# Who starts the first loads: weights on SP, biases and first rotary tables on ACT, two groups of dummy matmuls fewer

## The reference, cut to what matters

```
q = rope(x @ Wq + bq); k = rope(x @ Wk + bk); v = x @ Wv + bv      # 16 heads of 16
ctx = softmax(q k^T / 4) v
x = layernorm(x + ctx)
r = sigmoid(xr @ W_r^T); k = relu(xk @ W_k^T)^2; x = layernorm(x + r * (k @ W_v^T))
```

## Time and profile before

| | before |
|---|---|
| median of 3 runs | 1515.15 us (1514.39 to 1572.35) |
| profiled execution, its time | 1515.05 us |
| its span, first to last instruction | 1513.0 us |
| mean granted TensorE clock | 0.999 |
| PE busy | 1501.9 us, 99% |
| DVE, ACT, POOL busy | 1348.6, 1190.2, 347.0 us |

### The profile page before, as it was taken

How to read it: one execution, slowest core, us unless ns; L and a number is a source line. 1 busy time by engine, 2 the same in 40 slices (tenths; PEclk the granted TensorE clock), 3 DMA queues, 4 the chain that set the end, 5 groups by cost and what they waited for, 6 DMA issues and landing times.

```text
span 1513.0 us, 49359 instructions
## 1 busy us (share of the span) xinstructions
PE 1501.9 (99%) x21956; PEld 679.9 (45%) x21956; DVE 1348.6 (89%) x1453; ACT 1190.2 (79%) x2179; POOL 347.0 (23%) x348
## 2 busy tenths in 40 slices
PE   9999999999999999999999999999999999999998
PEld 3344444444444444444444444444444444443476
DVE  5669999999999999999999999999999999998597
ACT  3338888888888888888888888888888888888845
POOL 3510322132212212132213221042212000000175
PEclk9999999999999999999999999999999999999999
DMA  7825111121112100121112111101111212000133
GB/s 220 256 75 173 22 23 24 24 79 24 24 24 79 24 11 15 24 79 24 24 24 79 24 24 24 67 15 24 23 24 24 38 24 35 5 3 3 30 75 120
DMA packets 71957, 73.14 MB, mean 48 GB/s; under 512 B 47745, under 2 KB 57473, under 8 KB 69953
## 3 DMA queue, kind: packets, MB, share of 16 engines
q1 hardware_dynamic: 71200, 69.60, 20.1%
q10 hardware_dynamic: 544, 0.39, 0.1%
HBM read 29.07 MB, written 13.63 MB: 28 GB/s over the span
## 4 chain that ended last, share of the span: by engine, by line
PE 97%; DVE 1%; DMA 1%; ACT 1%; SPq 0%; issue 0%; POOL 0%; POOLq 0%; DVEq 0%; ACTq 0%
PE ring_ps L573 29%; PE score_ps L644 29%; PE pv_ps L592 29%; PE score_ps L547 2%; PE ring_ps L618 2%; PE score_ps L730 2%; PE score_ps L714 1%; PE pv_ps L714 1%; PE pv_ps L547 1%; PE score_ps L558 1%; DMA rope<-tables 0%; ACT probs L819 0%; DVE rope L1084 0%; PE pv_ps L558 0%; PE ring_ps L730 0%; DMA k_stack<-rope 0%
## 5 line engine op out<-in xcount | busy, mean ns | idle before, releaser
L1147 DVE TENSOR_REDUCE tile_max<-ring_ps 128x1 f32<-128x1024 f32 x1024 | 1207.3, 1215 | 116.3 <-PE ring_ps L573 111.2
L819 ACT ACTIVATE probs<-score_ps 128x512 f32<-128x512 f32 x2048 | 1109.9, 598 | 211.6 <-PE score_ps L644 153.5
L644 PE MATMUL score_ps<-q_stack,k_stack 99*32 99x512 bf16 x8192 | 715.5, 379 | 1.8 <-ACTq L807 0.8
L573 PE MATMUL ring_ps<-k_stack,q_stack 96*32 96x512 bf16 x8192 | 625.9, 378 | 0.4 <-DMA k_stack<-rope 0.4
L592 PE MATMUL pv_ps<-probs,v_aug 128*32 128x512 f32 x4096 | 532.0, 591 | 0.0
L573 PEld LDWEIGHTS ring_ps<-k_stack,q_stack 96*32 96x32 bf16 x8192 | 230.9, 96 | 331.1 <-issue 153.1
L644 PEld LDWEIGHTS score_ps<-q_stack,k_stack 99*32 99x32 bf16 x8192 | 227.7, 95 | 326.2 <-issue 150.1
L592 PEld LDWEIGHTS pv_ps<-probs,v_aug 128*32 128x32 f32 x4096 | 129.9, 110 | 98.2 <-ACT probs L819 0.3
L924 POOL TENSOR_TENSOR neg_cuts<-neg_max,zeros 128x16 bf16<-128x16 f32 x31 | 6.8, 219 | 533.8 <-DVE neg_max L1120 533.8
L916 POOL TENSOR_TENSOR v_aug<-v_all,b_v_s 128x256 f32<-128x256 f32 x32 | 23.2, 727 | 298.7 <-PE pv_ps L592 292.8
L937 POOL TENSOR_TENSOR ctx_part<-ctx_turn,recip 128x256 f32<-128x256 f32 x32 | 20.4, 636 | 237.1 <-DVE recip L1179 237.0
(11 more groups left out here) (108 smaller groups left out, 505.7 us busy)
## 6 DMA issues: line engine op xcount, KB each, us to landing
qk_raw<-probs SPq DMA_DIRECT2D x28, 256.0 KB, 3.7
rope<-qk_raw SPq DMA_DIRECT2D x7, 1024.0 KB, 4.8
rope<-qk_raw SPq DMA_DIRECT2D x14, 512.0 KB, 7.3
q_stack<-rope SPq DMA_DIRECT2D x31, 192.0 KB, 3.7
k_stack<-rope SPq DMA_DIRECT2D x31, 192.0 KB, 4.2
xz<-x_tok SPq DMA_DIRECT2D x2, 2048.0 KB, 12.2
q_stack<-rope SPq DMA_DIRECT2D x31, 128.0 KB, 3.7
k_stack<-rope SPq DMA_DIRECT2D x31, 128.0 KB, 3.7
```

Source lines behind the costliest of these rows:

```text
L573: mm = pe.matmul(ring_ps[k % 2][g:g + VCOLS, c * TOK:(c + 1) * TOK], q_stack[0:ROWS, buf, qt * P + g:qt * P + g + VCOLS], k_stack[0:ROWS, ...
L644: mm = pe.matmul(score_ps[n % SCORE_BANKS][g:g + VCOLS, :], k_stack[0:ROWS_M, h % STACKS, kt * P + g:kt * P + g + VCOLS], queries[:, j], s ...
L819: act.activation(probs[:, kt % 2, j, :], score_ps[n % SCORE_BANKS][:, :], ACT.Exp, scale=SCALE).then_inc(exps_done, 1)
L1147: dve.reduce_max(tile_max[:, h % 2, unit // 2, unit % 2:unit % 2 + 1], slot[:, :], AX.X)\
```

## The change

The first weights are no longer issued by ACT but by SP, ahead of everything else. ACT waits until they have landed and then issues the biases and tables 0, which SP issued before. SP's queue has one DMA more at its head and two fewer behind. The dummies go from seven groups of four matmuls to five. Nothing else is touched.

```diff
-WARM_UP = 7
+WARM_UP = 5
...
+            sp.dma_start(w_qk_s[:, :, 0:P], w_first).then_inc(w_first_in, DMA)
             for c, signal in enumerate((x_first_in, x_in[0])):
                 sp.dma_start(x_s[:, 0, c, :], x_blk[0, :, c, :]).then_inc(signal, DMA)
...
             sp.dma_start(w_v_s[:, :, :], w_v).then_inc(w_v_in, DMA)
-            sp.dma_start(b_qk_s[:, :], b_qk).then_inc(b_first_in, DMA)
             load_x(1)
-            load_tables(0)
             load_tables(1)
...
         def _(act):
-            act.dma_start(w_qk_s[:, :, 0:P], w_first).then_inc(w_first_in, DMA)
+            act.wait_ge(w_first_in, DMA)
+            act.dma_start(b_qk_s[:, :], b_qk).then_inc(b_first_in, DMA)
+            act.dma_start(tables_s[:, 0], tables[0]).then_inc(tables_in[0], DMA)
             act.wait_ge(b_first_in, DMA)
```

## The result

The changed kernel took 1517.67 us in the median of 14 runs (1515.73 to 1520.51), the kernel before 1514.95 us in 14 runs beside them. The ratio of the two is 1.0018, with a 95% interval of 1.0011 to 1.0025: slower by 2.7 us. Within the 2% of a "same" this is no change; against my forecast of +0.02 us and a range that ended at 1517.2 it is a miss. The one slow run of before, at 1572.35, is left out of the ratio, and without it the medians differ by 2.9 us.

What follows compares the result with a forecast made beforehand. PE was taken as the bound from the first maximum on, so its start decides: the stacks' wait goes, block 1's grows equally, +0.02 us. With 1515.05 profiled and the median 0.1 higher: 1515.1 us, range 1513.5 to 1517.2.

Steps and rivals of the forecast that it cites:

- What bounds the kernel: Up to the first maximum: PE's own chain and the one through tables 0 meet there, PE's only 0.37 us behind.
- 9.9 for block 1: Token block 1's landing: 9.9 us in place of 9.3, bounds 8.9 to 10.4, as it shares with tables 0.
- I take 9.9: Landing of tables 0 from ACT's queue: 9.9 us in place of 10.55, issued at about 4.5.
- My upper bound of 12.0: Landing of tables 0 on ACT's queue: issue at 4.5 plus the 7.45 us of before.
- Cost: nothing: First weights on SP: block 0 and w_v slide 0.5 to 0.65 us, hidden by the wait for block 1.
- Rival (b): Tables 0 late on ACT's queue, landing near 13.1 behind SP's loads; DVE's chain last, 2.5 us longer: 1517.6 us; chance 0.11.
- The dummies: Start of PE: two groups fewer remove 0.85 us of PE time in front of a wait, worth nothing.
- the sign that I named: PE's item 0 starts near 4.6 at full pace: 16 matmuls in 1.9 us is right, twice that wrong.
- Rival (c): PE's clock rises later; item 0 and first v at 1.2 GHz, first maximum 2.0 us later: 1517.1 us; chance 0.08.
- ACT's waits: Before ACT's first work: biases land at 7.8, 3.8 us after issue; v is ready at 8.5, so nothing is delayed.
- The sum: Whole kernel: 1515.05 profiled plus 0.02, and the median of the runs 0.1 higher: 1515.1 us, 0.0%.
- My last sign of being wrong: Behind 30 us: the prediction is wrong if anything there changes in length.

Runs made afterwards that it cites:

- e5: The kernel before with only the first weights moved, to the head of SP's queue; seven groups of dummies: 1515.54 us, ratio 1.0004.
- e3: The changed kernel with the biases back on SP's queue, behind w_v and ahead of block 1; ACT issues tables 0 alone: 1516.14 us, ratio 1.0008.
- e6: The kernel before with biases and tables 0 issued by ACT once the first weights, still on ACT, have landed; seven groups of dummies: 1518.67 us, ratio 1.0027.
- g2: Second profile of e6, nothing changed against it; a single run: 1518.64 us.
- g3: Second profile of e4, nothing changed against it; a single run: 1517.62 us.
- e4: The changed kernel with the two DMAs on ACT's queue swapped, tables 0 ahead of the biases: 1516.97 us, ratio 1.0012.
- f3: The kernel before, unchanged, run and profiled a second time: 1514.37 us, ratio 0.9995.
- e1: The kernel before with five groups of dummies in place of seven, all loads as before: 1515.76 us, ratio 1.0002.
- f2: The kernel before with two groups of dummies in place of seven, all loads as before: 1514.68 us, ratio 0.9999.
- e8: The changed kernel as it is, profiled a second time: 1517.00 us, ratio 1.0016 to the kernel before.
- g1: The changed kernel as it is, third profile; a single run: 1517.43 us.
- e2: The changed kernel with seven groups of dummies in place of five, its loads kept: 1517.17 us, ratio 1.0011.
- f4: The changed kernel with seven groups of dummies, profiled a second time (first profile: e2): 1517.13 us, ratio 1.0015.
- f1: The kernel before with tables 0 issued by ACT right behind the first weights, with no wait; biases stay on SP: 1514.47 us, ratio 0.9998.
- e7: The kernel before with the biases issued by ACT right behind the first weights, with no wait; tables 0 stay on SP: 1513.99 us, ratio 0.9994.

## Why the prediction was wrong

**What bounds the kernel: right, with some luck in the number.** Two chains meet at the first maximum, and what is late there reaches the end. PE's chain was predicted to 0.1 us (29.27 against 29.36), but its 9.9 for block 1 was reckoned from sharing with tables 0 alone. In e5, where only the first weights had moved, block 1 landed at 9.77 and 9.40, so the move of the weights, which I had put at nothing, was part of the 10.00. In the other two profiles of the changed kernel it was 10.49 and 10.36.

**The step that failed: "I take 9.9" for the landing of tables 0.** It measured 12.00, and 12.22 and 12.58 in the later profiles. Behind it stood an issue at 4.5 and 5.4 us of transfer; the issue came sooner, at 3.73, and the transfer took 8.27 us. I had reckoned that a second queue shares at once and that tables 0 and block 1 would end together, since the bytes ahead are the same. They were not: tables 1, 512 KB, were now issued ahead of tables 0. My upper bound of 12.0 hit the number by two errors that cancel, 4.5 + 7.45 for 3.73 + 8.27. What the runs showed in its place: in the changed kernel tables 0 pair with tables 1 and not with block 1. On one queue the loads of 512 KB land in the order of *issue*, mostly about 1.3 us apart; tables 0 on the other queue land 0.1 to 0.6 us from one that SP issued shortly before or behind them. Issue and landing in four kernels:

| | tables 0 | block 1 | tables 1 | block 2 |
|---|---|---|---|---|
| before | 3.10, 10.55 | 2.62, 9.26 | 3.57, 11.83 | 4.05, 13.11 |
| changed | 3.73, 12.00 | 3.06, 10.00 | 3.53, 11.56 | 4.01, 12.96 |
| e3 | 3.45, 11.29 | 3.52, 11.48 | 3.99, 12.73 | 4.47, 14.01 |
| e6 | 4.34, 14.29 | 2.14, 8.34 | 2.61, 9.60 | 3.08, 11.47 |

The queues do not run to this order by a rule: once the data of tables 0 flow, ACT's queue gets about half (51.6% against 51.3% in e3). And the order across the queues has exceptions: in e6 and g2 tables 0 landed 1.1 us ahead of block 3, and in g3 0.08 us ahead of block 1, though these had been issued 0.2 us before them. The step missed that ACT's queue gets data late. In the changed kernel hardly anything flowed on it before 6 us, 2.7 us after the issue of the biases, and then the biases' small pieces came first. How much of the 12.00 is the place behind tables 1 and how much the biases in front of tables 0 is not shown: e3 and e4 changed both at once, and no run issued the tables behind tables 1 without biases in front. How the engines are fed in that gap no view shows, so the order is a description of these runs, not an explanation.

The trace that I predicted from was also the latest of its kind. The four profiles with the loads of before (before, f3, e1, f2) have tables 0 at 10.55, 9.42, 9.85 and 9.14; the five with the changed loads (changed, e8, g1, e2, f4) have them at 11.79 to 12.58. In the means that is 2.4 us later, not 1.45.

**"Cost: nothing" for the first weights on SP: wrong by the landings.** I had the slide of block 0 and w_v right, but let block 1 be issued at 2.65 again. It was 3.06: I had charged one issue in front against one behind, and left out that the weights' issue takes 0.71 us and that block 0's two issues then take 1.05 in place of 0.87. e5 has the part alone: first maximum 30.0 in the mean of two profiles, against 29.0 in the four with the loads of before. Its +0.83 us in the medians fits, but its interval includes no change.

**The two parts don't add up, and shouldn't.** In the medians e5 costs 0.8 us, which is not clear of no change, and e6 4.0, together 2.7. On SP the weights land at 3.29 in place of about 3.9, so ACT issues tables 0 at 3.73 in place of 4.34, and SP's issues are later: one load of 512 KB that used to stand behind tables 0 is now issued ahead of them, where in e6 it is four, three of which also landed ahead. Moving the weights makes the wait for them cheaper.

**Rival (b) was the case, in the main.** It had DVE's chain the last again, its threshold of 10.6 us, and 1517.6 us against 1517.67. Its reason, that SP's loads are in effect served first, held for block 1 and tables 1 but not for block 2, which landed at 12.96, and f1 speaks against it as a rule. I gave it 0.11 because the first weights had landed in 3.6 us on ACT's queue. That row said nothing on it: they were issued within 10 ns of SP's first load, so nothing was ahead of them. The exact price is in part luck, since it came from a landing at 13.1 and the measured one is 12.0 plus, in part of the executions, the slower pace.

**The dummies: right in the cost, wrong in the sign that I named.** Item 0 started at 4.59, as said, but at 1.2 GHz pace (3.64 us in place of 1.92), which was to be the sign of being wrong. e1 and f2 cost nothing measurable, e2 gains nothing measurable. Rival (c) came closer than that suggests. Item 0 alone lost 1.7 us, more than the 1.4 us of cover. It cost nothing in this profile because v, from 7.98, took 2.02 us, nearly the 1.91 of full pace, and ended just as block 1 landed, at 10.0. In e8 and g1 v took 2.57 and 2.64 us as well, and in g1 PE took up block 1 at 10.79, 0.4 us after it had landed. That was hidden only because the stacks were later by another 2.0 us.

**ACT's waits: the size was off.** The biases landed at 9.47 and not at 7.8. The 3.8 us of the earlier trace rows were for a place on SP's queue behind block 0 and `w_v`, which landed 0.3 us before the biases; behind a wait, with 128 pieces of 20 bytes between SP's 4 KB pieces, they took 6.2 us here and 8.6 in e4. It cost nothing in the changed kernel, as v was ready only at 10.0 and tables 0 at 12.0, but it did in e4.

**The sum.** The three profiles of the changed kernel have the first maximum 2.4 us later than the two of before in the mean (31.4 against 29.0), and two of three have 1.8 us of slower pace behind it. My last sign of being wrong, that something behind 30 us changes in length, came true by that, and no term of the prediction stood for it. The medians differ by 2.3 to 2.7 us. I read this as mostly late tables, with a remainder from the pace in part of the runs; the share of each in the medians is not measured, as only profiled executions show it. The cause of the pace stays open: the dummies (e1, f2, f4) and tables 0 on ACT (e6, g2) are unlikely, the first weights on SP go with it in 10 and 8 profiles, and that is an association.

## What to carry to other kernels

When a load is moved to another queue, write down the moment of issue of every load on all queues and sort them: at a head that is full of loads, the place in that list is the first thing to look at, and a wait in front of an issue pays in whole loads that overtake (e6: 4.0 us). Without a wait the same large load on the second queue cost nothing (f1), and the small one neither (e7, whose gain is not shown). And a load moved to the head of a queue delays all behind it by its issue time, which for this one was 0.71 us, even where its own landing is hidden.

## What the runs showed of the hardware

- 2.5 KB in 128 pieces took 3.8 us to land on SP's queue behind block 0 and `w_v`, 6.2 us on ACT's queue behind a wait (changed), and 8.6 us behind a load of 512 KB there (e4).
- The 512 KB of tables 0 took 8.3 us (changed) and 9.95 (e6) from issue to landing, against 7.5 and 6.3 in two executions of the kernel before, for the same bytes.
- Two executions of the kernel before had block 1 at 9.26 and at 8.14 us with issues within 10 ns of each other: over a microsecond of chance in the head, more than several of the effects studied here, and only partly seen in the end (1515.05 and 1514.64 us).
- One program can run its heads at two paces, 0.13% apart. At the normal pace of the kernel before the matmuls of four column groups start within 25 ns of each other; in the first profile of the changed kernel they are spread over some 110 ns, and at the slower pace the weight loads' busy time was 1.6 to 1.8 times as long. Whether the spread alone costs the time is not shown: f1 had one of 212 ns at 1200 us, with the normal 1356.1 us, but only 34 ns at 500 and 800 us.
